# One transfer a tile for the attention bands, and outputs projected by units of every fourth token

## The reference

```python
# s: deformable attention. 16 heads of 16 features, 12 samples a query at fractional places within 8 tokens
off = tanh(pw_w @ gelu(depthwise_conv3(q_lin))) * 6.0
positions = clip(base + linspace(-2, 2, 12) + off, 0, q - 1)
sk, sv = sample(kh, positions), sample(vh, positions)       # linear interpolation of two neighbours
scores = (qh . sk) / sqrt(16) - rel_scale * abs(positions - base)
out = softmax(scores) @ sv                                   # 12 samples
s = out @ wo.T + bo
# g: mixture of 8 experts, top 2, hidden 512
g = silu(sum over the chosen experts of gate * (silu(a) * b) @ Wl2)
```

## Time and profile before

| | us |
|---|---|
| median of three runs | 1486.03 |
| the profiled execution, its own time | 1492.07 |
| its span, first to last instruction | 1489.9 |
| PE busy in the span | 1371.2 (92%) |
| DVE busy in the span | 1223.8 (82%) |
| mean granted TensorE clock | 0.961 of full |

### The profile page before, as it was taken

The page is one execution under the profiler, slowest core; times in us unless marked ns, Lnnn a source line. Parts: engine busy times, 40 slices in busy tenths (PEclk is TensorE's granted clock), DMA queues, the critical chain, the costliest instruction groups (busy, mean ns, idle before and its releaser), DMA issues. The chain is left out here.

```text
span 1489.9 us, 36039 instructions
## 1 busy us (share of the span) xinstructions
PE 1371.2 (92%) x13687; PEld 1094.2 (73%) x13688; DVE 1223.8 (82%) x1697; ACT 806.7 (54%) x1873; POOL 856.3 (57%) x566
## 2 busy tenths in 40 slices
PE   5998999986799999999999999999999967989897
PEld 4864565655688888888888888888888855767675
DVE  7846755555999899989989989999999998699731
ACT  2547677775455444545544454555444454665554
POOL 1001377784588877878788787888878442011111
PEclk9998999996899999999999999999999987989889
DMA  7943456777557586786758677685868588898886
GB/s 225 330 160 89 120 187 183 235 243 236 186 138 230 136 270 165 201 232 167 233 131 241 172 195 201 159 246 128 234 172 234 130 223 240 205 238 194 225 214 134
DMA packets 204250, 293.53 MB, mean 197 GB/s; under 512 B 25601, under 2 KB 161029, under 8 KB 203891
## 3 DMA queue, kind: packets, MB, share of 16 engines
q0 software_dynamic: 65792, 146.59, 38.6%
q1 hardware_dynamic: 135683, 144.84, 31.8%
q10 hardware_dynamic: 2672, 0.83, 0.2%
HBM read 182.83 MB, written 117.74 MB: 202 GB/s over the span
## 5 line engine op out<-in xcount | busy, mean ns | idle before, releaser
L1220 POOL DMA_INDIRECT moe_rows<-expert_mem,token_of x142 | 360.9, 2541 | 92.9 <-issue 52.8
L1488 PE MATMUL pA<-xsT,expert_mem 128*128 128x256 f32 x1136 | 261.4, 384 | 12.6 <-DMA expert_mem<-in_w_l 6.5
L1494 PE MATMUL pY<-expert_mem 128*128 x1136 | 264.2, 386 | 0.0
L1201 POOL DMA_INDIRECT expert_mem<-xn_rows,token_of x138 | 231.1, 1674 | 50.1 <-issue 47.0
L1488 PE MATMUL pB<-xsT,expert_mem 128*128 128x256 f32 x1136 | 256.8, 379 | 0.0
L1488 PEld LDWEIGHTS pA<-xsT,expert_mem 128*128 128x128 f32 x1136 | 218.2, 193 | 45.1 <-issue 9.0
L1494 PEld LDWEIGHTS pY<-expert_mem 128*128 128x128 f32 x1136 | 210.0, 190 | 41.8 <-issue 16.1
L1488 PEld LDWEIGHTS pB<-xsT,expert_mem 128*128 128x128 f32 x1136 | 215.8, 190 | 29.3
L1703 DVE SCALAR_TENSOR_TENSOR parts<-pos_pair,prob 128x768 f32<-128x768 f32 x224 | 197.7, 950 | 0.5
L1340 ACT ACTIVATE expert_mem<-pA,b1sel 128x256 f32<-128x256 f32 x284 | 111.2, 474 | 127.8 <-issue 123.9
L1349 ACT ACTIVATE expert_mem<-pB,b1sel 128x256 f32<-128x256 f32 x284 | 111.5, 475 | 110.7 <-PE pB L1488 110.7
(11 more groups left out here) (212 smaller groups left out, 2248.1 us busy)
## 6 DMA issues: line engine op xcount, KB each, us to landing
expert_mem<-in_w_l POOLq DMA_DIRECT2D x71, 1024.0 KB, 7.3
band<-band_rows SPq DMA_DIRECT2D x256, 96.0 KB, 3.7
S_rows<-expert_mem SPq DMA_DIRECT2D x64, 376.0 KB
band_rows<-wgt SPq DMA_DIRECT2D x12, 1536.0 KB, 7.4
pos_pair<-pos_rows SPq DMA_DIRECT2D x28, 384.0 KB, 5.7
xn_rows<-expert_mem SPq DMA_DIRECT2D x16, 512.0 KB, 5.6
v_rows<-expert_mem SPq DMA_DIRECT2D x16, 512.0 KB, 4.4
moe_rows<-zeros POOLq DMA_DIRECT2D x4, 2048.0 KB
```

Source lines behind the costliest of these rows:

```text
L1201: nc.gpsimd.indirect_dma_start(out=xs[:, u, s], out_offset=None, in_=dram["xn"], in_offset=bass.IndirectOffsetOnAxis(ap=keep["inv"][:, 2 * ...
L1220: nc.gpsimd.indirect_dma_start(out=dram["moe"], out_offset=bass.IndirectOffsetOnAxis(ap=keep["inv"][:, 2 * n + s:2 * n + s + 1], axis=0), ...
L1488: mm = nc.tensor.matmul(dst[:, c], w1[:, 1 - u, k, o * HID + c * P:o * HID + (c + 1) * P], xsT[:, k], start=(k == 0), stop=(k == KC - 1))
L1494: mm = nc.tensor.matmul(pY[:, s], hid[:, h, c, s * P:(s + 1) * P], w2[:, c, ds(e * D, D)], start=False, stop=(s == 1 and c == HC - 1))
```

## The change

Each tile's band now comes by one transfer. The skew is made when the bands are stored: `band_rows` has one row for each i with a pitch of 4 x 768 + 16 numbers (`BAND_PITCH`), and one transfer for each s stores a group, the last with 16 zeros more (`wgt` gets one more key for them). Reading 128 runs of 768 numbers without any skew then gives each row its shift.

Outputs are projected by units: `outT` holds four tiles twice over, and `project_unit` takes every fourth token of the unit before as its 128 columns, so that partition p gets tokens 4p to 4p+3, a run of 4096 bytes in the output and in `moe_rows`. The last unit keeps the old order, tile by tile. `outT` now lies in the shared memory, and `proj` has 8 slots instead of 10. In the front, the positions lose base and block in one instruction a tile instead of two. The tables are changed as shown.

```diff
-ROW_SLOTS = 10
+ROW_SLOTS = 8
-BAND_SKEW = SUBS * BAND - HEADS
+BAND_PITCH = SUBS * BAND + HEADS
-END_EXPONENT_AT = (0, 14, 28, 42)
-END_PREPARE_AT = (6, 21)
+END_EXPONENT_AT = (0, 17, 34, 50)
+END_PREPARE_AT = (8, 24)
-UNITS_AT = ({}, {5: 1, 7: 1}, {1: 1, 3: 1, 5: 1, 7: 1}, {1: 1, 3: 1, 6: 1}, {4: 1, 6: 1})
+UNITS_AT = ({}, {}, {0: 1, 2: 1, 5: 1, 7: 1}, {0: 1, 3: 1, 5: 1, 7: 1}, {1: 1, 4: 1})
...
-                    V.tensor_scalar(by_half[:, 0], by_half[:, 0], base_of(n, a), None, ALU.subtract)
-                    ins = V.tensor_scalar(by_half[:, 1], by_half[:, 1], base_of(n, a), float(WBLOCKS), ALU.subtract, ALU.subtract)
+                    ins = V.scalar_tensor_tensor(by_part, by_part, base_of(n, a), block_at[:].unsqueeze(2).broadcast_to([P, SAMPLES, HEADS]),
+                                                 ALU.subtract, ALU.subtract)
...
-        def band_of(n, s):
-            return bass.AP(dram["band"].tensor, (n * P + s) * BAND, [[BAND_SKEW, SUB], [1, BAND]])
+        def band_of(n):
+            return bass.AP(dram["band"].tensor, n * SUB * BAND_PITCH, [[BAND, P], [1, BAND]])
+        def weight_rows(group, s):
+            wide = BAND + HEADS if s == SUBS - 1 else BAND
+            rows = ds(group * GROUP * SUB, GROUP * SUB)
+            return (dram["band"][rows, s * BAND:s * BAND + wide].rearrange("(a i) c -> i a c", i=SUB),
+                    wgt[s:P:SUBS].rearrange("p a k h -> p a (k h)")[:, :, 0:wide])
         def unit_rows(t, k):
+            if k < LAST:
+                return t[k * GTOK:(k + 1) * GTOK, :].rearrange("(p a) c -> p a c", a=GROUP)
...
-                for s in range(SUBS):
-                    sp.dma_start(band[s:P:SUBS, f], band_of(n, s)).then_inc(band_loaded[f], 16)
+                sp.dma_start(band[:, f], band_of(n)).then_inc(band_loaded[f], 16)
...
-                if t >= 2:
-                    act.wait_ge(pj_done, t - 1)
+                k, a = t // GROUP, t % GROUP
+                if k >= 2 and a == 0:
+                    act.wait_ge(pj_done, GROUP * (k - 1))
...
-                if t > 0:
+                if GROUP <= t < LAST * GROUP:
+                    evacuate_proj(t - GROUP)
+                if t == LAST * GROUP:
+                    for a in range(GROUP):
+                        evacuate_proj(t - GROUP + a)
+                if t > LAST * GROUP:
                     evacuate_proj(t - 1)
...
+            def project_unit(i, a, u):
+                t = i * GROUP + a
+                pe.wait_ge(outT_ready, i * GROUP + GROUP)
...
+                    nc.tensor.matmul(pJ[a % 2], outT[:, u, c, a:GTOK:GROUP], wo[:, c], start=(c == 0), stop=False)
...
                     times_v(t, j, i)
-                    if not (first and j == 0):
-                        project(t - 1, (j + 1) % 2)
+                    if not (first or last):
+                        project_unit(i - 1, j, 1 - u)
+                    if last and j == 0:
+                        for a in range(GROUP):
+                            project_unit(i - 1, a, 1 - u)
+                    if last and j > 0:
+                        project_tile(t - 1)
```

More of the change, by code:

```diff
@@ L1003, in mix_block @@
         late_v = shared[:, W1_AT:W1_AT + LATE_F].rearrange("p (u s c) -> p u s c", u=2, s=SUBS)
[L1004 removed]
+        outT = shared[:, W1_AT + LATE_F:W1_AT + LATE_F + OUT_F].rearrange("p (u c n) -> p u c n", u=2, c=KC)
+        proj_at = W1_AT + LATE_F + OUT_F
+        proj = shared[:, proj_at:proj_at + ROW_SLOTS * UNIT_F].rearrange("p (k a c) -> p k a c", k=ROW_SLOTS, a=GROUP)
         wo = sb("wo", [P, KC, D])
@@ L1146, in store_weights @@
                 sp.wait_ge(w_ready, group + 1)
-                sp.dma_start(dram["band"][ds(group * GTOK, GTOK), :].rearrange("(a p) c -> p a c", p=P),
-                             wgt[:].rearrange("p a k h -> p a (k h)")).then_inc(w_stored, 16)
+                for s in range(SUBS):
+                    rows, some = weight_rows(group, s)
+                    sp.dma_start(rows, some).then_inc(w_stored, 16)
             def fill_out(it):
@@ L1268, in store_weights @@
                 pool.sem_inc(go, 1)
-                pool.dma_start(dram["band"][group * GTOK:(group + 1) * GTOK, :].rearrange("(a p) c -> p a c", p=P),
-                               wgt[:].rearrange("p a k h -> p a (k h)")).then_inc(end_w_stored, 16)
+                for s in range(SUBS):
+                    rows, some = weight_rows(group, s)
+                    pool.dma_start(rows, some).then_inc(end_w_stored, 16)
             def load_pos(it):
@@ L1585, in _, with four_tiles @@
             pe.wait_ge(ys_ready, SLOT_PAIRS)
-            def four_tiles(i, first=False, last=False):
+            def four_tiles(i, u, first=False, last=False):
                 for j in range(GROUP):
@@ L1593, in four_tiles @@
                     times_v(t, j, i)
-                    if not (first and j == 0):
-                        project(t - 1, (j + 1) % 2)
-            four_tiles(0, first=True)
-            with pe.Fori(1, TILES // GROUP - 1) as i:
-                four_tiles(i)
-            four_tiles(TILES // GROUP - 1, last=True)
-            project(TILES - 1, 1)
+                    if not (first or last):
[5 more added lines that the diff above has]
+                        project_tile(t - 1)
+            four_tiles(0, 0, first=True)
+            four_tiles(1, 1)
+            with pe.Fori(1, LAST // 2) as m:
+                four_tiles(2 * m, 0)
+                four_tiles(2 * m + 1, 1)
+            four_tiles(LAST - 1, 0)
+            four_tiles(LAST, 1, last=True)
+            project_tile(TILES - 1)
         @block.vector
@@ L1821, in build @@
         "bias": nc.dram_tensor("bias_parts", [NB, EXPERTS, 2 * D], BF16).ap(),
-        "band": nc.dram_tensor("band_rows", [TOKENS, BAND], F32).ap(),
+        "band": nc.dram_tensor("band_rows", [TILES * SUB, BAND_PITCH], F32).ap(),
     }
```

36 lines of the change are left out of this document (21 added, 15 removed).

## The result

| | before | the change |
|---|---|---|
| median, 20 runs each | 1485.03 us | 1492.63 us |
| lowest to highest | 1476.49 to 1494.83 | 1488.03 to 1498.63 |
| ratio | | 1.0053, 95% interval 1.0036 to 1.0071 |
| profiled execution, its span | 1492.07, 1489.9 | 1494.93, 1493.3 |

On another chip the change came out at 1.008 (1.006 to 1.0101). I had forecast 1463 us and a range of 1448 to 1480: wrong in sign, and outside the range.

What follows compares the result with a forecast made beforehand. SP's six transfer issues a tile were taken to set the tile stage's pace. Start 1222 + 44 tiles at 3.75 us + 79.6 gave a 1466.6 us span, 23.3 less, so median 1463 from 1486.0; range 1448 to 1480.

Steps and rivals of the forecast that it cites:

- to the last band done: Tile stage, last exponential to last band done: 34.0 us less one unit of 1.2 that falls in the wait, 32.8.
- tile 60 to the last product: Tail of PE's work: four projections instead of one add 3.8 us, restarting at half the clock 1.5.
- The pace: Tile stage to tile 50: 3.75 us a tile instead of 4.46, over 44 tiles; forecast case's chance 0.42.
- the same rate: 0: Projection's strided weight load: no added cost, at most 256 x 190 ns if doubled, which was left out.
- a pace of 3.55 to 3.91: Tile stage bounds: no burst felt, or four bursts of late bands fully felt, 16 us over 44 tiles.
- SP: Tile stage: three issues a tile instead of six save 1.9 us; a rule against it would keep the pace near 4.46.
- The late exponential: ACT's last exponential, after tile 50 at 1387, comes 26 us after DVE is ready and sets the end.
- My slower rival: One band transfer lands so late that the pace stays 4.46 and the late exponential costs: median 1494; chance 0.07.
- Four projections in the tail: After tile 60 the last unit does four projections where it did one: 3.8 us on the path.
- The last band: Before tile 60: issue 0.7, band store 10 and band load 3.7, together 14.4 us.
- Output stores: Stores in 4 KB runs: 2.8 us of all 16 engines instead of 4.3, 0.4 us of DMA a tile less.
- DMA's pace of 4.05: Rival, tile stage: DMA work and gaps between bursts set 4.05 us a tile, median 1476; chance 0.22.

Runs made afterwards that it cites:

- group 1: Edits to the change, one chip: neighbouring columns for the weight load, 1.0038; exponentials after tiles 0, 15, 30 and 42, 0.9923; both, 0.9891; plain output rows, 1.0005.
- Group 3: On one chip: the change again, 1.0080; the kernel before with one band transfer a tile, 0.9816; that with the change's tables as well, 0.9974.
- the band half: Kernel before with only one band transfer a tile and four skewed stores a group, old tables: ratio 0.9854, on another chip 0.9816 (1459.18 us).
- the band half with the same tables: Kernel before with one band transfer a tile, four skewed stores a group and all the change's tables, outputs in plain rows: ratio 0.9974.
- the second half: All the change has beyond band transfers and tables (strided load, long runs, four tail projections, front's edit), from ratios on one chip: +1.06%, 16 us.
- group 4: On one chip, the change with neighbouring columns for the weight load: with 4096-byte runs 1.0041, with plain rows 1.0028; 234.3 against 236.8 us to tile 60.
- the contiguous load: The change with ScalarE writing outT so that the weight load reads 128 neighbouring columns: 1493.21 us, ratio 1.0038 to the kernel before.
- the one with four band transfers: The change with four band transfers a tile and one store a group again, and exponentials after tiles 0, 15, 30 and 42: ratio 1.0074.

## Why the prediction was wrong, step by step

The sum had 1466.6 us of span; the profiled one is 1493.3, 26.7 more.

| term | predicted | measured | difference |
|---|---|---|---|
| last exponential, its table load | 1387 | 1408.9 | +21.9 |
| to the last band done | 32.8 | 32.9 | +0.1 |
| store, issue and load, to tile 60 | 14.4 | 16.6 | +2.2 |
| tile 60 to the last product | 25.2 | 23.6 | -1.6 |
| from there to the end | 7.2 | 11.3 | +4.1 |

**The pace was the step that failed.** "I take the middle with half a burst each and something for the clock, 3.75": in the sum's own terms it was (1408.9 - 1222) / 44 = 4.25, 0.50 us a tile more, 21.9 us in all. Two things are in that: by the undisturbed periods 7.5 us of weight load, and the rest, 14.4, that bursts cost more than was put down for them.

First, "the same rate: 0" for the strided weight load. It takes 329 ns instead of 190, and a tile 0.17 us more of PE's time, 7.5 us over 44 tiles. The bound of twice the time stood in the text and was left out of the range for a row that did not compare: the 96 columns in steps of eight belong to transpositions, not to f32 products, and even their rate was not the same, 1.67 ns a column against 1.48. Taking the cost away brought 3.9 us in group 1, which is hardly clear of chance; PE waited 2.5 us more for bands there.

Second, "a pace of 3.55 to 3.91" took four bursts as the worst, each for one late band with the old longest landing of 10.4 us, so 3.9 us a burst, and put down half. In the change the three bands issued from 1242 to 1249 landed after 10.4 to 13.2 us, those from 1305 to 1313 after 10.2 to 12.0, those from 1378 to 1386 after 10.7 to 13.4: three late bands in a row around each band store. PE's longer periods there add 5.8, 4.6 and 7.7 us. In 1222 to 1438 of the change 38 of PE's 51 periods last 3.69 to 3.82 us and 13 are longer; they add 24 us, of which 15.3 are gaps in PE's timeline, eight of them, and the rest goes mostly with work at the lower clock behind such a gap (8 transposes 1.63 us at 1396.35 instead of 1.11). The exponential, at 1408.9, carried nearly all of it to the end.

A page of the Trainium skill would have given the same zero for the weight load. TensorE: Matmul & The Clock Gate, section LDWEIGHTS (loading the stationary operand), makes its time a matter of the number of columns alone. The runs disagree: 189, 196, 259 and 324 ns for the same 128 columns.

**SP: right.** Three issues in 1.85 us, SP waits 130.7 us for PE, and the pace with plain weight loads fell from 4.56 to 4.07. The rule of the Trainium skill that the prediction weighed (DMA: Bandwidth & Descriptors, Issuing engines are not separate DMA queues), by which it would have stayed, is not borne out: with the same bytes, three issues less a tile moved it by half a microsecond. The edit takes away three transfers with the three issues, and no run takes the issues alone from SP; that it was the issues rests on SP's period of 3.86 us beside PE's 3.54, and on its waits.

**The late exponential: right, and its cost never named.** From the exponential to tile 60 the prediction had 47.2 us, and 49.5 were measured. PE reaches tile 60 after 29 of them (1438.25), so 20 us of waiting are in the measured time, and with 3.75 us a tile some 17 were in the sum. I saw that it sets the end and did not ask what the old place would give. Group 3 says it: the tables take 1.58% and the band half had brought 1.84%. Within the change the places 0, 15, 30 and 42 gained 1.3 to 1.5% (group 1). My slower rival named T = 4.29 as the point from which the change loses; 4.25 with the 2.2 and 4.1 us of the table is beyond it. The rival's reason, a band that lands no sooner, was not it: it held the slow pace possible only if the band transfer failed.

**Four projections in the tail: right.** In group 3 tile 60 to the last product is 23.6 us in the change and 20.3 in the band half with the same tables, 3.3 more against 3.8. The terms of that pair of traces, from the first silu on: pace 4.8, store and load to tile 60 1.2, tail 3.3, end 3.5, together 12.9 us of the second half's 16.

**The last band.** Its store took 7.5 us to the issue of tile 60's load where I had 10.7, but that load took 9.1 instead of 3.7, beside three output stores that DVE had kept behind its own wait for the exponential. That these stores slow it is argued, not tested by a run of its own. The traces go with it: in the three of the band half with the old tables the last output store had been issued 8.8 us or more before this load, and it took 3.1 to 3.6 us; in the eight with the late tables and one band transfer it took 7.7 to 9.1.

**Output stores: cheaper, by less than put down, and worth little.** POOL issues one in 0.87 us instead of 1.29 and it lands in 6.3 instead of 7.1 us. In 1420 to 1434, one store and one load (against the earlier trace rows):

```profile
q0 software_dynamic: 288, 1.05, 33.1%
```

That is 74 engine-us where it was 89, some 1 us of all 16 engines less a unit instead of the 1.5 in the forecast. The most that shows in a time is the 2.5 us of group 4.

**DMA's pace of 4.05:** the number came true for kernels with plain weight loads, the reason did not. The band half alone and the contiguous load run at 4.07 and 4.04 with shares of 0.93 and 0.79 in 1222 to 1438, so one pace comes with two shares, and between bursts PE does tile after tile in 3.54.

## What to carry to other kernels

Where a change brings new order tables, price them for themselves: ask what the old place would give at the new pace, not only whether the new one sets the end. An undisturbed period is not the pace; sum the long periods of the trace too, each with the slow stretch behind its gap, and count how many transfers in a row a burst makes late. And take the price of a strided operand only from a row of the same operation, or keep the doubled one in the range.

## What the runs showed of the hardware

- A weight load of 128 f32 columns takes 189, 196, 259 and 324 ns with steps of 1, 2, 3 and 4 numbers (4 to 16 bytes), in one kernel. ScalarE's write of 128 f32 columns in groups whose neighbours lie 512 bytes apart takes 481 ns instead of 364.
- All eight traces in which the first 15 units go by runs of 4096 bytes end late: 11.3 or 11.4 us after TensorE's last matmul in seven, 10.5 in the one with four band transfers, against 7.2 to 8.2 in the nine others, though the last four stores are the same. In the change the last transfer is issued at 1483.57 and lands some 3 us later; from 1486.8 on GpSimd's DRAIN takes 6.28 us. It takes 6.28 in seven traces with the long runs and 5.42 with four band transfers, against 2.03 to 2.97 in the nine others. Why it is longer behind transfers with long runs stays open.
- Chips differ: two of those used took some 150 us longer in the front of this program (the first expert product starts at 516 to 520 us instead of 359 to 369) and hardly in the last stage (total of the band half alone: 238.4 and 241.1 us).
